# A graph network on one core: how TensorE announces its products in the edge sums

## The reference, cut to what matters

```python
edge_index = jnp.stack([src, dst])
xn = _layernorm(x, axis=-1)
x = x + _L0_gnn_ref(xn, edge_index, ...) + _L0_mix_ref(xn[None], ...)[0]
x = x + _L0_ffn_ref(_layernorm(x, axis=-1)[None], ...)[0]
xn = _layernorm(x, axis=-1)
x = x + _L1_gnn_ref(xn, src, dst, ...) + _L1_mix_ref(xn[None], ...)[0]
x = x + _L1_ffn_ref(_layernorm(x, axis=-1)[None], ...)[0]

# inside the graph attention (layer 1 with 8 heads, layer 0 with one)
e = jax.nn.leaky_relu(a1[src] + a2[dst], negative_slope=ALPHA)
m = jax.ops.segment_max(e, dst, num_segments=n)
ex = jnp.exp(e - m[dst])
s = jax.ops.segment_sum(ex, dst, num_segments=n)
alpha = ex / s[dst]
out = jax.ops.segment_sum(ft[src] * alpha[:, :, None], dst, num_segments=n)
```

## Time and profile before

| | us |
|---|---|
| median of 3 runs | 1890.13 |
| lowest and highest run | 1889.97 to 1891.54 |
| span of the profiled execution (no time of it beside the span is shown) | 2276.6 |
| first gather of layer 0's edge sum to its last product | 67.9 to 744.4 |
| first gather of layer 1's edge sum to its last product | 1176.1 to 1932.7 |

### The profile page before, as it was taken

One profiled execution on the slowest core, in us unless ns is written; L12 is line 12 of the kernel. 1 busy time (PEld: TensorE's weight loads), 2 busy tenths in 40 slices (PEclk: granted clock), 3 DMA queues, 4 the chain that ended last, 5 costly groups with the idle time before them and its releaser, 6 DMA issues. The chain is left out here.

```text
span 2276.6 us, 34460 instructions
## 1 busy us (share of the span) xinstructions
PE 1646.4 (72%) x9468; PEld 1342.0 (59%) x9468; DVE 1163.6 (51%) x3309; ACT 656.1 (29%) x2160; POOL 1009.6 (44%) x1093
## 2 busy tenths in 40 slices
PE   5177776677778978999463665777577777689991
PEld 4045555556656557999343554555455556689991
DVE  7256566555456664222452555556566657841223
ACT  4222121122322554333152222332222212643330
POOL 4556555656543002555124545555454541325550
PEclk9588888889889989999786777888787989599996
DMA  7323222333222016666532222222222220267666
GB/s 167 98 71 84 80 75 75 87 82 87 78 70 58 1 63 224 211 213 210 135 112 72 80 74 77 74 80 75 70 77 68 72 72 20 93 199 213 215 202 178
DMA packets 148002, 244.24 MB, mean 107 GB/s; under 512 B 53369, under 2 KB 83368, under 8 KB 147558
## 3 DMA queue, kind: packets, MB, share of 16 engines
q0 software_dynamic: 48384, 134.19, 21.1%
q1 hardware_dynamic: 97306, 106.27, 15.7%
q10 hardware_dynamic: 2124, 1.54, 0.3%
HBM read 210.48 MB, written 31.21 MB: 106 GB/s over the span
## 5 line engine op out<-in xcount | busy, mean ns | idle before, releaser
L679 POOL DMA_INDIRECT es_rows<-table,eall x784 | 745.7, 951 | 719.3 <-SPq L668 418.6
L699 PE MATMUL bank<-es_msg,es_one 128*125 128x264 f32 x976 | 305.3, 466 | 123.5 <-DVE es_msg L822 104.1
L699 PE MATMUL bank<-es_rows,es_won 128*125 x976 | 289.8, 448 | 116.8 <-DVE es_won L819 84.8
L762 ACT ACTIVATE es_oneT<-bank 125x512 bf16<-125x512 f32 x244 | 145.1, 595 | 755.9 <-remote 488.5
L699 PEld LDWEIGHTS bank<-es_msg,es_one 128*125 128x125 f32 x976 | 209.0, 225 | 175.2 <-DVE es_msg L822 113.9
L699 PEld LDWEIGHTS bank<-es_rows,es_won 128*125 128x125 f32 x976 | 202.4, 218 | 159.2 <-issue 125.3
L842 DVE TENSOR_TENSOR es_z<-es_rows,es_near 128x4 f32<-128x4 f32 (+1 forms) x244 | 43.1, 177 | 359.3 <-ACTq L774 265.2
L1237 PE MATMUL bank<-ffn_xbT,ffn_w 128*128 128x128 f32 x1792 | 220.8, 277 | 0.0
L1290 ACT ACTIVATE xT<-bank,ffn_b1s 128x128 f32<-128x128 f32 x448 | 128.2, 369 | 303.2 <-PE bank L1237 292.6
L1396 DVE TENSOR_TENSOR xT<-bank,xT 128x256 f32<-128x256 f32 x112 | 47.6, 425 | 327.8 <-issue 190.1
L1247 PE MATMUL bank<-ffn_w,xT 128*128 x896 | 211.7, 379 | 0.0
(11 more groups left out here) (445 smaller groups left out, 2408.8 us busy)
## 6 DMA issues: line engine op xcount, KB each, us to landing
ffn_w<-in_L_ffn_W SPq DMA_DIRECT2D x112, 512.0 KB
es_rows<-table,eall POOLq DMA_INDIRECT x784
ffn_w<-yrows SPq DMA_DIRECT2D x20, 560.0 KB
ffn_w<-in_L_ffn_W SPq DMA_DIRECT2D x2, 4096.0 KB
xrows<-acc SPq DMA_DIRECT2D x10, 560.0 KB
table<-acc SPq DMA_DIRECT2D x5, 577.5 KB
table<-acc SPq DMA_DIRECT2D x5, 564.4 KB
out_x<-xs SPq DMA_DIRECT2D x5, 560.0 KB
```

The lines of the kernel that those rows point to most:

```text
L679: pool.indirect_dma_start(rows[:, q % R, w, :], None, m.table[H], bass.IndirectOffsetOnAxis(ap=m.eall[:, at:at + 1], axis=0)).then_inc(gat ...
L699: ins = pe.matmul(sum_banks[p % 2][0:P, 0:W], left, right, start=(w == 0), stop=(w == BW - 1))
L762: a.activation(oneT[:, p % 2, :], turn_bank[0:P, :], ACT.Copy).then_inc(kept, 1)
```

## The change

The increments leave the products of the three parts of a step. After the turn PE gets one drain (an instruction that waits until the engine has finished what was issued) and then increments the three semaphores with instructions of their own, and the mixture's products move behind that. In the mixtures each announcement moves from the last product to a drain behind it.

```diff
-                        ins = pe.matmul(sum_banks[p % 2][0:P, 0:W], left, right, start=(w == 0), stop=(w == BW - 1))
-                    ins.then_inc(summed, 1)
+                        pe.matmul(sum_banks[p % 2][0:P, 0:W], left, right, start=(w == 0), stop=(w == BW - 1))
...
-                        ins = pe.matmul(scores_of[p % 2][:, w, :], oneT[:, p % 2, w * 128:(w + 1) * 128],
+                        pe.matmul(scores_of[p % 2][:, w, :], oneT[:, p % 2, w * 128:(w + 1) * 128],
                                         stage[:, p % 4, :], start=True, stop=True)
-                    ins.then_inc(scored, 1)
...
-                        ins = pe.matmul(at, flags, ident[:, :], start=True, stop=True)
-                    ins.then_inc(turned, 1)
+                        pe.matmul(at, flags, ident[:, :], start=True, stop=True)
 
                 for i in range(STEPS + 4):
                     if valid(i - 4):
                         sums(i - 4)
                     if valid(i - 2):
                         scores(i - 2)
-                    side.tensor(pe, i)
                     if valid(i):
                         turn(i)
+                    pe.drain()
+                    if valid(i - 4):
+                        pe.sem_inc(summed, 1)
+                    if valid(i - 2):
+                        pe.sem_inc(scored, 1)
+                    if valid(i):
+                        pe.sem_inc(turned, 1)
+                    side.tensor(pe, i)
```

In `Mix0.tensor` and `Mix1.tensor` every group that ended in `ins.then_inc(...)` is changed alike; the two matmuls with zeros that close a sum keep their increment. One of the 20 places:

```diff
             for k in range(KD):
                 ins = pe.matmul(m.bank[4 + 3 * (t % 2)][0:P, :], m.xT[:, k, tile_cols(t)], m.wkv[:, k, :], start=(k == 0), stop=(k == KD - 1))
-            ins.then_inc(self.made, 1)
+            pe.drain().then_inc(self.made, 1)
```

More of the change, by code:

```diff
@@ L1707, in tensor @@
                                 start=False, stop=False, skip_group_check=True)
-            ins.then_inc(self.summed, 1)
+            pe.drain().then_inc(self.summed, 1)
         for t in self.key(i):
@@ L1725, in tensor @@
                 ins = pe.matmul(m.bank[7][:, k * 128:(k + 1) * 128], self.wide[:, k, :], m.ident[:, :], start=True, stop=True)
-            ins.then_inc(self.spread, 1)
+            pe.drain().then_inc(self.spread, 1)
         if i == 2:
@@ L1732, in tensor @@
                     ins = pe.transpose(m.bank[7][:, at:at + 128], m.wq[:, b, k * 128:(k + 1) * 128], m.ident[:, :])
-            ins.then_inc(self.qturned, 1)
+            pe.drain().then_inc(self.qturned, 1)
         if i == self.FOLD:
@@ L1737, in tensor @@
                 ins = pe.transpose(m.bank[7][:, k * 128:(k + 1) * 128], m.kv[:, k, :], m.ident[:, :])
-            ins.then_inc(self.flipped, 1)
+            pe.drain().then_inc(self.flipped, 1)
         if i == self.FOLD + 2:
@@ L1743, in tensor @@
                 ins = pe.matmul(m.bank[4][:, k * D:(k + 1) * D], self.kvT[:, k, :], m.w1[:, k, :], start=True, stop=True)
-            ins.then_inc(self.joined, 1)
+            pe.drain().then_inc(self.joined, 1)
         if i == self.FOLD + 4:
@@ L1754, in tensor @@
                                     start=(k == 0), stop=(k == KD - 1))
-            ins.then_inc(self.mapped, 1)
+            pe.drain().then_inc(self.mapped, 1)
         for t in self.output(i):
@@ L1761, in tensor @@
                 ins = pe.matmul(m.bank[4 + 3 * (t % 2)][0:P, 0:D], m.xT[:, k, tile_cols(t)], m.w2[:, k, :], start=(k == 0), stop=(k == KD - 1))
-            ins.then_inc(self.out, 1)
+            pe.drain().then_inc(self.out, 1)
         for t in self.hide(i):
@@ L1771, in tensor @@
                                     start=(k == 0), stop=(k == KD - 1))
-            ins.then_inc(self.hidden, 1)
+            pe.drain().then_inc(self.hidden, 1)
         for b in range(KD):
@@ L1779, in tensor @@
                     ins = pe.transpose(m.bank[5 + 2 * (u // 4)][:, (u % 4) * 128:(u % 4 + 1) * 128], m.gn[:, u, b * 128:(b + 1) * 128], m.ident[:, :])
-                ins.then_inc(self.gturned, 1)
+                pe.drain().then_inc(self.gturned, 1)
     def scalar(self, a, i):
@@ L1981, in tensor @@
                     ins = pe.transpose(m.bank[4 + 3 * (g % 2)][0:D // 4, at:at + P], m.tail[:, t, HEADS:], m.ident[0:P, 0:P])
-                ins.then_inc(self.zturned, 1)
+                pe.drain().then_inc(self.zturned, 1)
         if i == 1:
@@ L2015, in tensor @@
                 ins = pe.transpose(m.bank[4 + 3 * (t % 2)][0:P, k * 128:(k + 1) * 128], self.ekT[:, s, k, :], m.ident[:, :])
-            ins.then_inc(self.turned, 1)
+            pe.drain().then_inc(self.turned, 1)
         if i == self.CLOSE:
@@ L2032, in tensor @@
                                     m.wqkv[:, b, 2 * D + k * 128:2 * D + (k + 1) * 128], start=(b == 0), stop=(b == KD - 1))
-            ins.then_inc(self.crossed, 1)
+            pe.drain().then_inc(self.crossed, 1)
         if i == self.FOLD + 4:
@@ L2057, in tensor @@
                                     start=(k == 0), stop=(k == KD - 1))
-            ins.then_inc(self.queried, 1)
+            pe.drain().then_inc(self.queried, 1)
     def scalar(self, a, i):
```

## The result

The changed kernel takes 1967.77 us (median; 1966.43 to 1975.89) beside 1890.84 us for the kernel before: a ratio of 1.0409, 95% interval 1.0386 to 1.0432. It is 77 us slower. The forecast was 32 us slower; the measured time lies inside the range given.

The account below looks back on a forecast made before the run. The gathers were taken to bound the kernel at 494 us a stage; the drains would raise PE to 513 and 527 us, +52, or +13 at full clock. The middle, +32, gave 1922 us, range 1825 to 2010.

Parts of the forecast that it names:

- the main drain with its increments: On PE behind each turn: 0.37 to 0.72 us a step, taken as 0.6, or 146 us over 244 steps.
- the mixture's drains: On PE at 243 mixture announcements: 0.21 to 0.40 us each, taken as 0.35, or 85 us.
- The granted clock: PE's clock share in the edge sums, 0.84 and 0.81 in the profile, taken as 0.95 after the change.
- the move at nothing: Mixture's products moved behind the turn: turn announced 1.17 us earlier less the drain, said to gain nothing at the gathers' pace.
- rival of hidden drains: Drains fall into PE's wait for DVE's weights and POOL keeps the pace: 1890 us within 3; chance 0.20.
- The later announcement of the scores: Scores announced some 0.23 + 0.6 us later, said to lie in DVE's slack: nothing, or 0.8 us a step without slack.
- a stage's sum of PE work: PE's work in each edge sum plus drains, 513 and 527 us, against the gathers' 494: +52 us.
- PE's load: PE's own work in the two edge sums before the change: 383 and 386 us, or 403 and 406 at clock 0.95.
- The equality 2276.6 - 385 = 1892: Profile span less POOL's true waiting matches the runs' median, read as edge sums running at the gathers' pace.
- Late increments as real time: Rival: late increments in the edge sums cost time without the profiler too and the change ends them: 1850 us; chance 0.27.
- A drain that is held: Rival: what holds the increment back also holds PE's drain or the increment behind it: 2050 us; chance 0.09.
- The announced signs: In the profile after: 0.4 to 0.7 us from drain's end to next product, ACT's copy right behind its increment, no releaserless waits.

Follow-up runs that it names:

- e7: The changed kernel with every fourth gather of a block replaced by a plain transfer issued by SP: 1969.05 us, ratio 1.0412 to the kernel before.
- e11: The changed kernel with two more semaphore increments a step, for which nobody waits: 2035.55 us, ratio 1.0745 to the kernel before.
- e4: The changed kernel with the increments of sums, scores and turn back on their products, both kinds of drain kept: 1911.22 us.
- e1: The kernel before with only the mixture's products moved behind the turn, no drains, increments on products: 1853.00 us, ratio 0.9786.
- e12: The changed kernel with the mixture's products put back between scores and turn, all drains and increments kept: 2053.54 us, ratio 1.0862 to the kernel before.
- second profile: The kernel before, unchanged, profiled once more: the profile spans 1891.6 us, the run took 1893.32 us.
- e6: The kernel before with every fourth gather of a block replaced by a plain transfer issued by SP: 1878.44 us, ratio 0.9926.

## Why the prediction was right about the sign and wrong about the size

**Right: what the drains cost PE.** Foreseen were 0.6 us for the main drain with its increments, 146 us in all, and 85 us for the mixture's drains, 231 together; read from the products' starts they are 0.54 to 0.69, 142, 86 and 228. The bound of 0.72 for one main drain held. Of the pieces, an increment costs 0.15 us, three times its duration of 51 ns, where twice had been allowed; but only two instructions follow the drain, so that their 0.27 us kept within the 0.30 allowed for three. The granted clock, taken at 0.95, was 0.94 and 0.97. That the added time of PE would make PE the bound, and not the gathers, was right as well: e7 gains nothing, and e11 pays for PE time alone.

The Trainium skill, PSUM — Partial Sum Buffer, section "Engine vs sequencer instructions", has the rule to attach the increment to the producing matmul, as a matter of correctness. In time the runs here speak for the same choice, with 0.27 us for a drain and 0.27 for what follows it: putting the main increments back on their products, with all drains kept, takes 60 us off the change, and taking the drains away as well another 58 (e4 and e1 in the table).

**Wrong: the move at nothing.** The step failed at "The turn is announced earlier by the mixture's products [...]. In the gathers' pace that buys nothing either." The move is worth 41 us alone and 84 in the whole change. The evidence stood in the rows: PE's idle 0.86 us before the sums of 1507.40 was released by DVE, and the prediction read it, in its rival of hidden drains, as room, instead of following it back over ACT's `ready` to the turn and to the mixture's products in front of it. The later announcement of the scores was put at nothing too, as lying in DVE's slack; DVE's waits for them rose from 20.7 to 115.7 us, and what that costs is open.

**Wrong: how PE's added time becomes time of the kernel.** The prediction compared a stage's sum of PE work, 513 and 527 us, with the pace of 494, and charged only what lies above. By that the drains would add 52 us at a clock of 0.95, 13 at full clock, and it took the middle, 32. Without the move they add 161 (e12), 0.71 of their PE time; with it 118. The sum over a stage has no place for a step whose PE work is all on its loop; the eight slots, as I read it, even out POOL and not the loop of PE, ACT and DVE. PE's load itself was put too low: 403 and 406 us before the change, where the second profile has 428.8 and 427.8 busy. With these the same sum would have given about 100 us in place of 52, by the same faulty rule.

These two errors pull in opposite directions: 161 for the drains less 84 for the move is the measured 77. With the move's worth added to the forecast and the drains left as they were, it would have come out as faster (32 - 84), on the wrong side. The right sign is therefore in part luck.

**Wrong: the premise.** The equality 2276.6 - 385 = 1892 took a disturbed execution as the program plus a delay that one could subtract. That it came out within 2 us was luck: the same sum on the second profile gives 1891.6 - 20 = 1871 us. It named nearly the right state of POOL, which waits some 20 us in a good profile, and led to the wrong conclusion that the gathers set the pace of the runs: the edge sums of the kernel before last 521.6 and 527.8 us, not 494, and a quarter fewer gathers gain 12 us (e6). The gathers' pace is real as a floor: the order-only kernel stands on it, with 499.8 and 510.2 us for stages put at 494.

**The rivals.** Late increments as real time fell: the second profile has none, and its span is its runs' time; there ACT starts 0.04 us after the turn's end (1401.41 against 1400.97 + 0.40), so increments on products are prompt, against what the prediction read from the earlier trace rows. Hidden drains fell by the table above, though the order-only kernel hides three quarters of a first one. A drain that is held fell: the gaps behind the turn are 0.53 us, with nothing of several us among them.

**What would show it.** The announced signs came out as 0.53 us between the turn and the next product and as ACT's copy L766 released by PE's new instruction:

```profile
  PEq L729: 404.3, 219
  PEq L725: 0.9, 2
```

No wait is without a releaser. But the sum is larger than in the second profile of before (362.4): the turn is announced late by the drain and two increments, and all that the order gains at ACT (179.7 by itself) is given away again. The profile's span came close to its runs, as announced, but so did that of the kernel before at its second execution; the change did not do it.

## What to carry to other kernels

Before an engine's idle time is counted as room, follow its releaser back: if the chain returns to the same engine, the idle time is part of a loop, and work put on that loop is paid in large part (0.71 of it in e12), while work taken off it can be won (41 us here). Announce a product that others wait for before issuing products that nobody waits for yet, and leave the increment on the product. The best kernel found here is the order alone, at 1853 us against 1890 and 1968; a change made of several parts is worth taking apart, since the one with the gain may be hidden under those with the losses.

## What the runs showed of the hardware that was not expected

A profiled execution can be 20% longer than the runs of the same program without any sign in its head: 2276.6 us against 1890, and 1891.6 at the second try. Its mark was an engine's waits without a releaser, 488.5 us in 81. Its length next to the runs' median is the first thing to look at, and a second profile is worth more than an argument about where the surplus lies.

PE's own semaphore increments are 51 ns long in the trace and cost 0.15 us each: two more of them in each of 244 steps made the kernel some 66 us slower, although nobody waited for them. Of three written behind a drain only two appear as instructions (L727, L729), so that one rides on the drain.
